# Attention b's tokens read back in four pieces by batches, with the first batch's statistics alone ahead of its steps

## The reference

```python
x = x + attn_a(layernorm(x))      # 16 heads of 8, log-sparse mask, biases
x = x + ffn(layernorm(x))         # each token to one of 8 experts by its affinity
x = x + attn_b(layernorm(x))      # 16 heads of 64, causal mask
x = x + ffn(layernorm(x))         # the same experts again
# layernorm: (x - mean) / sqrt(var + 1e-5) over a token's 128 numbers
```

## Time and profile before

| what | us |
|---|---|
| median of 3 runs | 565.84 |
| lowest and highest of them | 563.9 and 568.18 |
| the profiled execution, its own time | 566.51 |
| its span in the profile | 564.7 |

### The profile page before, as it was taken

The page is one execution under the profiler, slowest core; times in us unless marked ns, Lnnn a source line. Parts: engine busy times, 40 slices in busy tenths (PEclk is TensorE's granted clock), DMA queues, the critical chain, the costliest instruction groups (busy, mean ns, idle before and its releaser), DMA issues.

```text
span 564.7 us, 10428 instructions
## 1 busy us (share of the span) xinstructions
PE 461.5 (82%) x3500; PEld 362.5 (64%) x3500; DVE 374.8 (66%) x1091; ACT 228.8 (41%) x835; POOL 235.9 (42%) x245
## 2 busy tenths in 40 slices
PE   3957895715989179999999999999999997419993
PEld 2324554614989046777787877878787785319993
DVE  6598976851666347767768687696777955345772
ACT  2720001501444006555646466366564564104451
POOL 5002784471444314433435334363444624322453
PEclk9987998555999669999999999999999999758998
DMA  8999600034464200000000000000000000116560
GB/s 296 403 422 420 277 1 1 15 109 136 142 176 148 77 1 2 1 1 2 1 1 2 2 1 11 11 20 1 2 11 11 21 0 1 39 62 178 155 201 19
DMA packets 21878, 47.73 MB, mean 85 GB/s; under 512 B 3233, under 2 KB 13480, under 8 KB 19394
## 3 DMA queue, kind: packets, MB, share of 16 engines
q1 hardware_dynamic: 18818, 40.73, 20.7%
q0 software_dynamic: 3008, 6.34, 3.3%
HBM read 23.82 MB, written 24.15 MB: 85 GB/s over the span
## 4 chain that ended last, share of the span: by engine, by line
PE 69%; DVE 10%; POOL 8%; DMA 5%; issue 5%; ACT 2%; POOLq 0%; SPq 0%; ACTq 0%; DVEq 0%
PE ps L888 10%; PE ps L917 9%; PE ps L964 8%; PE ps L951 7%; PE ps L833 7%; PE ps L846 6%; PE ps L905 5%; PE ps L895 5%; PE ps L923 3%; POOL sum L441 3%; DMA pv<-in_w 2%; POOL sorted_in L466 2%; PE ps L681 2%; POOL sum L445 2%; PE ps L787 1%
## 5 line engine op out<-in xcount | busy, mean ns | idle before, releaser
L495 POOL TENSOR_TENSOR vT<-vT,prec 128x256 f32<-128x256 f32 (+1 forms) x128 | 103.1, 825 | 157.5 <-DVE prec L1373 157.4
L632 ACT ACTIVATE vT<-ps,nmax 128x128 f32<-128x128 f32 (+1 forms) x256 | 105.1, 434 | 27.8 <-DVE nmax L1365 27.8
L640 ACT COPY prod<-ps 128x384 f32<-128x384 f32 x96 | 42.9, 481 | 111.3 <-PE ps L951 108.3
L1365 DVE TENSOR_REDUCE nmax<-ps 128x2 f32<-128x256 f32 (+1 forms) x128 | 62.3, 548 | 25.6 <-PE ps L923 25.6
L888 PE MATMUL ps<-xnT,wb 128*128 128x256 f32 x256 | 67.9, 389 | 4.6 <-DVE xnT L1345 3.9
L951 PEld LDWEIGHTS ps<-cst,vT 128*128 128x128 f32 x384 | 44.7, 140 | 18.8 <-issue 14.5
L632 ACT ACTIVATION_READ_ACCUMULATOR vT<-ps,nmax 128x1 f32 x256 | 55.9, 218 | 0.0
L951 PE MATMUL ps<-cst,vT 128*128 128x128 f32 x384 | 52.5, 273 | 1.8 <-POOL vT L495 1.7
L888 PEld LDWEIGHTS ps<-xnT,wb 128*128 128x128 f32 x256 | 44.8, 195 | 10.8 <-DVE xnT L1345 4.3
L917 PE MATMUL ps<-qk 64*128 64x128 f32 (+1 forms) x512 | 51.2, 339 | 0.0
L964 PE MATMUL ps<-prod 128*64 128x256 f32 (+1 forms) x512 | 50.0, 338 | 1.4 <-ACT prod L640 1.4
(11 more groups left out here) (152 smaller groups left out, 829.8 us busy)
## 6 DMA issues: line engine op xcount, KB each, us to landing
sorted_in<-zero SPq DMA_DIRECT2D x1, 16512.0 KB, 59.2
pv<-in_w SPq DMA_DIRECT2D x30, 259.0 KB, 2.8
pv<-sorted_in SPq DMA_DIRECT2D x46, 129.0 KB, 2.5
wps<-in_w SPq DMA_DIRECT2D x1, 2072.0 KB, 10.1
w2s<-in_w SPq DMA_DIRECT2D x1, 2048.0 KB, 13.8
wb<-in_w_b SPq DMA_DIRECT2D x1, 1536.0 KB, 18.0
xres<-in_x SPq DMA_DIRECT2D x4, 256.0 KB, 3.6
xres<-after_ffn SPq DMA_DIRECT2D x4, 256.0 KB, 3.8
```

The lines of the kernel that those rows point to most:

```text
L495: last = nc.gpsimd.tensor_tensor(px, px, view(prec, m_at(n, x) + t * 2, [[1, 2], [0, (t + 1) * P]]), ALU.mult)
L632: last = nc.scalar.activation(pb[:, o:o + (t + 1) * P], wide[:, c:c + (t + 1) * P], ACT.Exp, bias=nmax[:, m:m + 1], accum_out=psum[:, m:m ...
L640: nc.scalar.copy(pT[:, c:c + BLOCKS * P], bank[hh][:, 0:BLOCKS * P]).then_inc(b_pa, 1)
L1365: last = nc.vector.tensor_reduce(nmax[:, m:m + 2], view(wide, x * 1024 + t * P, [[512, 2], [1, (t + 1) * P]]), AX.X, ALU.max, negate=True)
```

## The change

A constant names four pieces of the batches: 0 alone, 1 to 3, 4 and 5, 6 and 7. SyncE issues eight reads, one for each piece and half (two of 64 KB, two of 192 KB, four of 128 KB), both halves of a piece on one semaphore. Ahead of the steps VectorE makes the statistics of batch 0 alone (two tiles), normalises it, and goes on. The statistics of batches 1 to 3 (six tiles) stand at the end of step -2, those of batches 4 and 5 (four tiles) at the end of step 0, those of 6 and 7 (four tiles) at the end of step 1. GpSimd takes the powers of two and six columns ahead of its steps, now behind its waits on `f_ld`, and those of four columns behind its divisions in steps 1 and 2. `norm_b` waits for the power of its own batch; the wait for both powers ahead of the steps is gone.

```diff
@@ -41,6 +41,7 @@
 DHB = 64
 NPAIR = HB // 2
 STEPS = NPAIR // 2
+RELOAD = ((0, 1), (1, 4), (4, 6), (6, 8))
 RING = 4
 BLOCKS = 3
 MASKED = -1e30
@@ -412,8 +413,9 @@
             slots(0)
             wait_all(sp, f_st, 0, NSLOT)
             bv = x_dram.rearrange("(b t p) d -> t p b d", p=P, t=T)
-            for i in (0, 2, 1, 3):
-                sp.dma_start(xr[:, 4 * i:4 * i + 4, :], bv[i // 2][:, i % 2 * 4:i % 2 * 4 + 4, :]).then_inc(in_x[i], 16)
+            for i, (lo, hi) in enumerate(RELOAD):
+                for t in range(T):
+                    sp.dma_start(xr[:, t * NB + lo:t * NB + hi, :], bv[t][:, lo:hi, :]).then_inc(in_x[i], 16)
             slots(1)
             wait_all(sp, f_st, 1, NSLOT)
 
@@ -481,10 +483,11 @@
                 dispatch(0, g)
             for s in range(NSLOT):
                 give_back(0, s, x_dram)
-            for q in range(2):
+            def powers_b(q):
+                lo, n = RELOAD[q][0], RELOAD[q][1] - RELOAD[q][0]
                 pool.wait_ge(n_ve, q + 1)
-                nc.gpsimd.tensor_tensor(view(rstd, 4 * q, [[NB, T], [1, 4]]), view(veps, 4 * q, [[NB, T], [1, 4]]),
-                                        view(mhalf, 0, [[4, T], [1, 4]]), ALU.pow).then_inc(n_rs, 1)
+                nc.gpsimd.tensor_tensor(view(rstd, lo, [[NB, T], [1, n]]), view(veps, lo, [[NB, T], [1, n]]),
+                                        view(mhalf, 0, [[n, T], [1, n]]), ALU.pow).then_inc(n_rs, 1)
 
             def divide(b, j):
                 n = (b, j)
@@ -499,6 +502,8 @@
             def step(b, j):
                 n = (b, j)
                 divide(b, j)
+                if n in ((0, 1), (0, 2)):
+                    powers_b(j + 1)
                 h, d = group_at(n)
                 if 0 <= h < NG - 1 and d == 2:
                     powers(1, h)
@@ -509,6 +514,8 @@
 
             for i in range(XR):
                 pool.wait_ge(f_ld[i], landed(1, i, XR))
+            powers_b(0)
+            powers_b(1)
             all_steps(step, 0, 0)
             dispatch(1, NG - 2)
             powers(1, NG - 1)
@@ -1327,8 +1334,14 @@
             nc.vector.tensor_scalar(wb[:, 0:HB * DHB], wb[:, 0:HB * DHB], float(DHB) ** -0.5, None,
                                     ALU.mult).then_inc(b_w, 1)
 
+            def statistics_b(q):
+                lo, hi = RELOAD[q]
+                dve.wait_ge(in_x[q], 48)
+                statistics([t * NB + b for t in range(T) for b in range(lo, hi)], [[NB, T], [1, hi - lo]], n_ve)
+
             def norm_b(b):
                 need(dve, b_xT, b)
+                dve.wait_ge(n_rs, 1 if b == 0 else 2 if b < 4 else 3 if b < 6 else 4)
                 for t in range(T):
                     last = nc.vector.tensor_scalar(xn[:, t * D:(t + 1) * D], xtile(b, t),
                                                    mv[:, bass.ds((t * NB + b) * 2, 1)],
@@ -1403,6 +1416,8 @@
                     residual_b(b - 1)
                 if j == 0 and some(b) and some(b + 1):
                     norm_b(b + 1)
+                if n in ((-1, 2), (0, 0), (0, 1)):
+                    statistics_b(nth(n) + 2 if b == 0 else 1)
                 h, d = group_at(n)
                 if 0 <= h < NG - 1:
                     if d == 0:
@@ -1419,14 +1434,8 @@
                     if d == 6:
                         place(1, h)
 
-            for q in range(2):
-                dve.wait_ge(in_x[q], 32)
-                dve.wait_ge(in_x[q + 2], 32)
-                statistics([t * NB + 4 * q + i for t in range(T) for i in range(4)], [[NB, T], [1, 4]], n_ve)
-                if q == 0:
-                    dve.wait_ge(n_rs, 1)
-                    norm_b(0)
-            dve.wait_ge(n_rs, 2)
+            statistics_b(0)
+            norm_b(0)
             dve.wait_ge(f_sent, NT * 16)
             nc.vector.tensor_copy(view(pack, 2 * D + 1, [[GT * ROW, NG], [2 * ROW, T], [ROW, 2]]),
                                   view(cst, C_TOKEN, [[2, NG], [NB, T], [1, 2]]))
```

## The result

| | median us | lowest and highest | runs |
|---|---|---|---|
| before | 567.01 | 563.9 and 569.57 | 4 |
| changed | 559.32 | 557.46 and 564.56 | 4 |

The ratio of changed to before is 0.9888, with a 95% interval of 0.9843 to 0.9934. The forecast was 559.5, in a range of 557.2 to 562.8. A later series (12 runs of the changed kernel, 29 of before) gave 559.07 against 565.14, a ratio of 0.9900 (0.9865 to 0.9934), so 5.6 us less. Faster is settled; whether by more or less than 1% is not, since both intervals hold 0.99.

What follows compares the result with a forecast made beforehand. TensorE bounds the kernel, but the change lies in its idle gap before attention b's first projection, where every term is on the path. 6.98 us off less 0.68 given back is 6.3: 565.84 - 6.3 = 559.5 us, range 557.2 to 562.8.

Steps and rivals of the forecast that it cites:

- The copy no longer waits for batches 4 to 7: VectorE's copy of batch 0's transposes follows them directly, so the first projection starts at 198.94, not 202.37: 3.43 us off.
- Two tiles for eight: Ahead of batch 0 VectorE makes statistics of six tiles fewer, 1.17 and 0.41 us: together 1.58 us off.
- A power of two columns: GpSimd's power ahead of batch 0 takes about 0.73 us, 0.94 off; 0.63 off if floored at four columns.
- The landing: The first 64 KB reads of attention b land at 191.6 in place of 192.62, 1.03 us off.
- the bound of 2.0: Quickest landing allowed, from the kernel's quickest 129 KB read, 2.0 us: landing at 191.29, 1.33 us off.
- The first projection: Attention b's first projection on TensorE comes at 195.4 in place of 202.37, four terms summing to 6.98 us off.
- Given back: Moved statistics in VectorE's list delay TensorE 0.48 us in step -2 and about 0.2 in step 0: 0.68 us.
- The slow stretch of the clock: After the first projection TensorE's clock stays at 0.50 for the same 6.2 us as before; no gain or loss.
- The rival of the sooner clock: Clock rises sooner after the first projection, up to 1.0 us better: 558.2 to 559, about 558.5; chance 0.20.
- The split does nothing: Rival: eight smaller reads share engines and the first pair still lands at 192.6: 560.5 us; chance 0.17.
- Paid in full: Rival: moved statistics all delay TensorE, 4.9 us in place of 0.68: 563.7; chance 0.12, including more than half paid.
- The clock stays down: Rival: a TensorE break in attention b's first steps keeps the clock at 0.50, 14 us further giving about 566.5; chance 0.04.

Runs made afterwards that it cites:

- the finer statistics: Changed kernel with batch 1's statistics alone in step -2, batches 2 and 3, 4 and 5, 6 and 7 in steps 1, 2, 3: 559.19 us, ratio to before 0.9891.

## Why the prediction was right

The forecast was 6.3 us off, and 559.5. The first pair of medians differs by 7.7, the longer series by 6.1 (its ratio, 5.6). By the traces, and that is the better measure of the change itself, the steady steps come 6.8 to 6.9 us earlier; the longer series shows up to 1.3 us less, which its interval (3.7 to 7.6 us) allows and nothing here explains. That 559.5 met 559.32 to 0.2 us is luck: the sum started from 565.84, and with the fourth run the median before was 567.01.

**The copy no longer waits for batches 4 to 7, 3.43 us.** Right: 3.44 when it was made alone.

**Two tiles for eight, 1.58 us.** Right: 1.66 + 0.66 - 0.50 - 0.26 = 1.56.

**A power of two columns, 0.94 us off.** Right: 0.73 us where eight columns took 1.67. There is no floor at four columns.

**The landing, 1.03 us off.** Right in kind, too small: the start of the statistics moved from 3.87 to 2.34 us behind the issue, 1.53 us. The step that failed took the first 256 KB read's 2.9 us less the bytes, 2.3 us. The second small read was used 1.93 us after its issue (1.90 to 2.00 in three traces), at or below the bound of 2.0 that I had set as well, which came from reads of 129 KB. The profile lists the 64 KB reads at 1.8 us from issue to landing, and the 192 KB ones at 2.7. The Trainium skill's figures in "DMA: Bandwidth & Descriptors" (Anatomy of one DMA), given for another issuing path, made an estimate of 2.15 us, which was nearer than mine and still long. The Trainium skill's rule in the same page (Rules for kernel authors), to coalesce small transfers, did not decide: the split was worth 1.3 to 1.5 us, because TensorE waits here for the first landing and not for the bytes.

**The first projection, 6.98 us earlier.** It was 7.36 (13.53 to 6.17). The four terms as measured give 3.44 + 1.56 + 0.94 + 1.53 = 7.47; most of the 0.1 between is a gap of 0.17 us ahead of the power that was 0.08. It is there when only the order is changed, too; what makes it was not tried.

**Given back, 0.48 + 0.2 us.** Right. TensorE's wait behind the first maxima grew by 1.18 - 0.70 = 0.48 us. From first to second group of values it is 7.76 us and was 7.62, so 0.14 in step 0; step 1 gave nothing back, 7.40 as before. From the first projection to the third values the first pair of traces has 33.08 and was 32.66: 0.42 in all, against 0.68. But in this pair the slow stretch is 0.4 us shorter after the change, and TensorE reaches the third group of projections 7.58 us behind the first where it took 7.75: of the 0.48, 0.17 are the clock's. Where the slow stretches agree the price shows whole: the finer statistics, with a stretch of nearly the same length, take 31.64 us from the first projection to the third values where the changed kernel's second trace takes 32.20, so 0.56 us, of which 0.44 fall in step -2 and 0.12 in step 0. The maxima behind step 0's statistics came 0.52 us late and not 0.65, and the point at which TensorE paid was not the one forecast: it was the copy of queries and keys (L1363, 0.06 us ahead of the projections that need it), and not L1359, on which TensorE did not wait. The divisions were early enough, as taken, by 0.11 us.

**The slow stretch of the clock, unchanged.** Right on average. It lasted 6.2, 4.0 and 5.9 us before and 5.8, 3.8 and 6.2 after. Two us less of it were worth 0.87 us before and 0.8 after. The rival of the sooner clock exists, in one of three traces of either kernel, and so it does not come with the change. By the prediction's own words a slow stretch much other than 6 us was a sign of being wrong; 3.8 us in the second trace was that, and it cost the forecast nothing because the kernel before has it too. TensorE's gap ahead of the transposes was 8.68 us, where the forecast said 9.4 and its own terms give 12.62 - 3.55 = 9.07.

**The other rivals.** "The split does nothing" falls by 1.4 us. "Paid in full" (4.9 us) falls by the finer statistics and by the 0.42 to 0.6 that were paid. "The clock stays down" in the first steps was never seen. What I had not written down is that the clock falls at the other end of attention b, for 0 to some 11 us, and is worth up to 4 us there. That, the second ffn (61.5 to 64.3 us) and the time up to the reads (187 to 191) make the spread between these traces of either kernel; the first two are why the first profile showed 1.9 us of a gain of 6.9.

## What to carry to other kernels

Where an engine's list mixes the work of the first item with that of all, cut out what the first item needs and put the rest where that engine waits anyway, each piece no larger than the idle time read at that place: 0.93 us in a gap of 1.51 cost nothing, 1.99 cost 0.4 to 0.5. Cut the transfer in the same way if the first landing is what is waited for. And when one profile shows a fraction of the gain, measure it between landmarks around the change before looking for a loss.

## What the runs showed of the hardware

Four reads of 256 KB and eight of 64 to 192 KB bring the same megabyte, but the first pair is usable 1.5 us sooner, and SyncE issues the eight in 3.89 us where the four took 2.05. A GpSimd power in float32 took 0.73, 1.04, 1.33 and 1.67 us for 2, 4, 6 and 8 columns. Extra matmuls in a gap of TensorE's held the clock at 1.00 across it, with 0.6 and 0.5 us left idle around the transposes, and that brought the steady steps 2.7 us forward; but in its profiled execution the clock then fell for some 10 us at a place about 270 us later, and its median shows less than the traces promise. Whether the two are linked stays open: of the four traces with extra matmuls two have the long fall and two have none.
